# First preparation of a cross-attention and expert kernel written as its own program: new order of stages, weights in halves, output weight in quarters

## The chip, the cores and the metric

The kernel runs on one NeuronCore of a Trainium2 chip. The metric is device time in microseconds (us) of one execution. The kernel before took 869.69 us, the median of three runs (866.67 to 873.19 us).

TensorE (PE) multiplies, VectorE (DVE), ScalarE (ACT) and GpSimd (POOL) do elementwise work, and SyncE (SP) issues most transfers. Each engine works through its own program in order, and the engines meet only in semaphores: an instruction that waits holds up all that stands behind it on its engine.

## The reference, cut to what matters

```python
# B=8 batches, L=112 tokens, D=512, 16 heads of 32; context of 375 rows: 257 image, 118 text
h   = layernorm(x)
q   = rms_norm(h @ q_w.T + q_b) * norm_q_w
k   = rms_norm(ctx_txt @ k_w.T + k_b) * norm_k_w
ki  = rms_norm(ctx_img @ k_img_w.T + k_img_b) * norm_k_img_w
v, vi = ctx_txt @ v_w.T + v_b,  ctx_img @ v_img_w.T + v_img_b
x   = x + (attention(q, k, v) + attention(q, ki, vi)) @ o_w.T + o_b
h   = layernorm(x)                        # then 8 experts, the 2 best of each token:
x   = x + sum_e gate_e * (gelu(gelu(h @ W1_e) @ W2_e) @ W3_e)
```

All is float32 in and out. Products keep float32 accuracy with three matmuls each: every operand is split in a high part, rounded to the type fp32r, and a low part, the rest, and high*high, high*low and low*high are summed.

## The kernel before

**Stages.** `bodies` (L263) runs the body of each engine for b = -1 to 8. In the body of b an engine works on the attention of batch b, on the preparation of batch b + 1 (queries, keys, values), and on the output, gate and routing of batch b - 1. The body of b = -1 holds a preparation alone; that is the first preparation, the one that is changed. After the bodies come the expert blocks, from weights that are loaded as the blocks run. Each body has 16 steps (h = 0 to 15, one per head), and tables say at which step a piece of preparation stands: `FILL` for PE, `EVACUATE_AT` for ACT, `SQUARES_AT` for POOL. The order is written by hand; no scheduler moves anything.

**Names of the preparation.** `xT`: transposes of the normalised x. `qt`, `kt`: the queries (112 tokens) and text keys (118 rows), 12 matmuls of 512 columns each, which ACT copies to `xn` and PE transposes back (`q`, `kx`). `k0` to `k3`: image keys, 12 matmuls of 258 columns each. `v0` to `v2`: values, 12 matmuls of 512 columns each. `ms`: sums over squares for the RMS norm; POOL then raises them to the power -0.5 and `rb` spreads the result. All these tiles of PE go through two PSUM banks in turns (`tile_use`).

**Weights.** Six attention weights of 1 MB arrive as float32 in two buffers (`raw_w`, L167). ACT rounds each to its high part (`split_weights`, L552), DVE subtracts it for the low part (`split_weights`, L734). Their order is image keys, text keys, queries, image values, text values, output (`ORDER`); the first two are split ahead of the body of b = -1, the others in it at steps 2, 7, 11 and 15 (`WEIGHTS_AT`). The context of batch 0 is split by ACT and DVE (L559, L722). On PE the body of b = -1 does k0, k1, kt, kx, xT, qt, k2, q, k3, v0, v1, ms, rb, v2, and last the values of the last image keys (L1238 to L1240), which go to `vlast_d` in memory and come back as one row per batch.

**Other transfers.** SP (from L277) issues weights 1 and 2 with the first context between them, then x of batch 0; each later weight waits until its buffer has been split. Behind these stand x and context of batch 1, then eight stores of zeros (`slots_d`, L313, 528 KB each), and the store of `vlast`. DVE waits for all eight stores at the end of step 0 of batch 0. POOL issues four small loads (`obr`, `wgs`, `bgr`, `b12s`, L399 to L402) at the start.

**The way into batch 0.** DVE finishes the queries and the first chunk of keys (`normalise_queries`, `normalise_keys`, then the low parts into `kq`, L805 and L801), PE makes the first scores (L1140), and DVE takes their maxima (L811), behind which the exponentials of ACT stand.

## Time and profile before

| | |
|---|---|
| median of three runs | 869.69 us (866.67 to 873.19) |
| the profiled execution, its own time | 870.31 us |
| its span in the trace | 868.5 us |
| busy: PE, weight loads of PE, DVE, ACT, POOL | 88%, 77%, 70%, 57%, 27% |
| chain that ended last: PE, DVE, ACT, issue, DMA | 72%, 11%, 7%, 5%, 1% |
| TensorE clock granted, mean | 0.942 of full |

Of each row of the profile the time is the start from the span's begin; "busy" counts instructions, not how full the engine is. The chain of waits is followed back from the last instruction: at each step to what released it. Matmuls are shown with modelled ends, so the distance from one start to the next says more than one's own duration.

### The profile page before, as it was taken

The page shows a single profiled execution, that of the slowest core. Times are in us where ns is not written, and L with a number is a line of the kernel's source. Part 1 is how long each engine was busy: PE and PEld are TensorE (multiplying, and loading weights), DVE is VectorE, ACT ScalarE, POOL GpSimd, SP SyncE. Part 2 cuts the span into 40 slices and gives each one's busy share as a digit, 9 for nine tenths or more (in the row PEclk, how much of TensorE's full clock was granted, in tenths as well). Part 3 has the DMA queues.
Part 4 walks back from the last instruction along what each step waited for, and adds up shares of the span by engine and source line. Part 5 has one row for each costly group of instructions (what it writes and reads, how often), then busy time and mean ns, then how long its engine had stood idle before and what let it go on. Part 6 is the DMA issues. An engine that isn't in the chain of part 4 may idle for free.

```text
span 868.5 us, 17362 instructions
## 1 busy us (share of the span) xinstructions
PE 767.1 (88%) x5934; PEld 668.7 (77%) x5934; DVE 603.7 (70%) x1276; ACT 495.2 (57%) x1131; POOL 231.2 (27%) x286
## 2 busy tenths in 40 slices
PE   3879898999999999764299999999999999999991
PEld 2657676767776767543299999999999999999991
DVE  5476878787878787657166768676767767676853
ACT  4366777777777777682044645554555455454640
POOL 3232334343433333104710303021111112030301
PEclk9999999999999999665599999999999999999996
DMA  6631001020202010405845565656665657565663
GB/s 217 251 135 55 22 38 53 39 65 27 66 26 72 20 43 3 180 21 220 300 157 194 212 216 194 255 174 251 212 247 175 250 198 259 179 246 187 222 213 125
DMA packets 28929, 130.68 MB, mean 150 GB/s; under 512 B 4316, under 2 KB 4332, under 8 KB 17872
## 3 DMA queue, kind: packets, MB, share of 16 engines
q1 hardware_dynamic: 23264, 114.26, 37.3%
q0 software_dynamic: 5616, 15.81, 5.1%
q8 instruction: 26, 0.43, 0.2%
q14 instruction: 23, 0.19, 0.1%
HBM read 113.14 MB, written 19.01 MB: 152 GB/s over the span
## 4 chain that ended last, share of the span: by engine, by line
PE 72%; DVE 11%; ACT 7%; issue 5%; DMA 1%; POOL 1%; SPq 0%; ACTq 0%; DVEq 0%; POOLq 0%
PE tiles L1040 7%; PE tiles L1042 7%; PE tiles L1041 7%; PE scores L1304 4%; PE scores L1302 4%; PE scores L1303 4%; PE ptb L1150 4%; PE ptb L1040 3%; PE ptb L1041 3%; PE ptb L1042 3%; PE pvb L1042 3%; PE pvb L1040 3%; PE pvb L1041 3%; PE pvb L1173 2%; PE scores L1140 2%
## 5 line engine op out<-in xcount | busy, mean ns | idle before, releaser
L834 DVE TENSOR_TENSOR w<-scr,w 128x2048 fp32r<-128x2048 f32 x76 | 174.1, 2291 | 69.9 <-ACT w L624 69.9
L624 ACT ACTIVATE w<-scr 128x2048 fp32r<-128x2048 f32 x76 | 144.8, 1907 | 60.7 <-PE scores L1304 59.3
L470 POOL DMA_INDIRECT out_dram<-scr,tok x18 | 36.5, 2030 | 301.1 <-DVE scr L1030 298.4
L606 ACT ACTIVATE scr<-scr,rsum 112x257 f32<-112x257 f32 x128 | 66.4, 519 | 62.8 <-DVE rsum L818 62.7
L1040 PE MATMUL tiles<-c,w 128*128 128x256 f32 (+1 forms) x272 | 81.3, 299 | 18.1 <-DVE c L722 15.5
L1042 PE MATMUL tiles<-w 128*128 128x256 f32 x288 | 81.5, 283 | 0.0
L1041 PE MATMUL tiles<-w 128*128 128x256 f32 x288 | 81.5, 283 | 0.0
L1040 PE MATMUL tiles<-w 128*128 128x256 f32 x288 | 81.5, 283 | 0.0
L1150 PE MATMUL ptb<-ident,scr 112*128 112x112 f32 x384 | 65.2, 282 | 18.3 <-ACT scr L614 16.6
L1042 PE MATMUL tiles<-c,w 128*128 128x256 f32 (+1 forms) x272 | 78.7, 289 | 0.0
L1041 PE MATMUL tiles<-c,w 128*128 128x256 f32 (+1 forms) x272 | 78.7, 289 | 0.0
L1150 PEld LDWEIGHTS ptb<-ident,scr 112*128 112x128 f32 x384 | 44.5, 149 | 42.5 <-ACT scr L606 26.7
L1018 DVE CAST w<-scr 128x256 fp32r<-128x256 f32 x144 | 44.0, 306 | 43.1 <-ACT scr L690 43.1
L614 ACT ACTIVATE scr<-ptb 128x336 f32<-128x336 f32 x128 | 57.4, 449 | 24.4 <-PE ptb L1150 24.3
L1040 PEld LDWEIGHTS tiles<-c,w 128*128 128x128 f32 x272 | 53.7, 197 | 20.1 <-issue 19.7
L690 ACT ACTIVATE scr<-tiles,b12s 128x256 f32<-128x256 f32 x72 | 33.2, 472 | 57.3 <-PE tiles L1042 57.2
L1020 DVE TENSOR_TENSOR w<-scr,w 128x256 fp32r<-128x256 f32 x144 | 61.3, 426 | 4.9
L598 ACT ACTIVATE scr<-scores,nmax 112x257 f32<-112x257 f32 x128 | 62.3, 486 | 2.5 <-DVE nmax L812 2.5
L1302 PE MATMUL scores<-w 128*128 128x512 f32 x144 | 56.9, 395 | 0.0
L811 DVE TENSOR_REDUCE nmax<-scores 112x2 f32<-112x514 f32 x64 | 44.0, 687 | 18.0 <-PE scores L1140 18.0
L1304 PE MATMUL scores<-w 128*128 128x512 f32 x144 | 56.2, 390 | 0.0
L1303 PE MATMUL scores<-w 128*128 128x512 f32 x144 | 56.1, 390 | 0.0
(214 smaller groups left out, 2291.4 us busy)
## 6 DMA issues: line engine op xcount, KB each, us to landing
scr<-in_dram SPq DMA_DIRECT2D x86, 1024.0 KB, 4.8
scr<-in_dram SPq DMA_DIRECT2D x8, 750.0 KB, 4.6
scr<-slots_d SPq DMA_DIRECT2D x10, 528.0 KB, 3.7
slots_d<-rows SPq DMA_DIRECT2D x8, 528.0 KB, 11.6
xn<-in_dram SPq DMA_DIRECT2D x10, 256.0 KB, 3.1
xb<-in_dram SPq DMA_DIRECT2D x8, 224.0 KB, 2.9
xr<-in_dram SPq DMA_DIRECT2D x8, 224.0 KB, 2.5
out_dram<-x SPq DMA_DIRECT2D x8, 224.0 KB, 2.8
```

Source lines behind the costliest of these rows:

```text
L598: act.activation(probs[0:L, s, 0:IMG], scores[0:L, s, 0:IMG], ACT.Exp, bias=nmax[0:L, g, s, 0:1], accum_out=sums[0:L, g, s, 0:1])
L606: act.activation(probs[0:L, s, 0:IMG], probs[0:L, s, 0:IMG], ACT.Copy, scale=rsum[0:L, g, s, 0:1]).then_inc(S["normal_img"], 1)
L624: act.activation(EH[slot], raw[slot], ACT.Copy).then_inc(S["eh_done"], 1)
L834: dve.tensor_tensor(EL[slot], raw[slot], EH[slot].bitcast(F32), ALU.subtract).then_inc(S["el_done"], 1)
L1020: dve.tensor_tensor(hL[lay][:, c, :], gel[:, m % 4, :], hH[lay][:, c, :].bitcast(F32), ALU.subtract).then_inc(S["hl_done"], 1)
L1040: pe.matmul(out, wh, xh, start=start, stop=False)
L1041: pe.matmul(out, wh, xl, start=False, stop=False)
L1042: return pe.matmul(out, wl, xh, start=False, stop=stop)
L1150: mm = pe.transpose(ptb[:, t * L:(t + 1) * L], probs[0:L, h % 4, t * P:(t + 1) * P], ident[0:L, 0:L])
L1302: pe.matmul(yb[:, t, :], h_hi, wh[:, i, :], start=(f == 0), stop=False)
L1303: pe.matmul(yb[:, t, :], h_hi, wl[:, i, :], start=False, stop=False)
L1304: mm = pe.matmul(yb[:, t, :], h_lo, wh[:, i, :], start=False, stop=(f == 7))
```

## The change

The first preparation is taken out of `bodies` and written as a function `first` for POOL, ACT, DVE and PE, and as straight code for SP; the body of b = -1 is gone.

- Order on PE: xT, qt, kt (half), q, kt, k0, kx, k1, k2, k3, v0, v1 (half), ms, v1, rb, v2.
- Order of the weights: queries, text keys, image keys, image values, text values. They arrive and are split in halves of 512 KB, in three buffers; the third is the start of `scr`, the keys and values of the odd batches.
- SP issues x of batch 0 first, then the query weight, the context, and the rest.
- POOL, not ACT, makes the high part of the first context. Its four small loads stand behind that.
- The output weight is loaded in quarters of 256 KB into `x1` and `rows`, and is split in batch 0: ACT at steps 1, 2, 8 and 9, DVE at steps 2, 3, 9 and 10. Two quarters are issued ahead of the eight stores of zeros, two in batch 0 behind the context of batch 2.
- The values of the last image keys are made in batch 0, step 0, behind the first scores; their store stands there too.
- All squares, adds and norms keep their engines.

The diff, without unchanged lines that say nothing and with the indentation cut by eight; of removed blocks the first two lines stand:

```diff
-ORDER = (WKI, WK, WQ, WVI, WV, WO)
-WEIGHTS_AT = {2: 2, 7: 3, 11: 4, 15: 5}
+ORDER = (WQ, WK, WKI, WVI, WV)
+BIG_FIRST = ("qt", "kt", "k0", "k1", "k2", "k3", "v0", "v1", "v2")
+OUT_HIGH_AT = {1: 0, 2: 1, 8: 2, 9: 3}
+OUT_LOW_AT = {2: 0, 3: 1, 9: 2, 10: 3}
...
-    if b <= FIRST:
+    if b < FIRST:
+        g = BIG_FIRST.index(name)
+    elif b == FIRST:
         g = (each - 1) * (b - FIRST + 1) + i - (i > o)
...
-vlast = rows[0:B, 0, 0:D]
+vlast = xr[0:B, :]
...
-raw_w = [scr[:, probs_at + i * PIECE:probs_at + (i + 1) * PIECE] for i in range(2)]
+raw_w = [scr[:, i:i + PIECE] for i in (probs_at, probs_at + PIECE, 0)]
+raw_o = [x1[:, :], rows[:, 0, 0:D]]
+side = lambda ap, k: ap[:, k * PIECE // 2:(k + 1) * PIECE // 2]
+quarter = lambda ap, c: ap[:, c * D:(c + 1) * D]
...
-    for b in range(-1, DONE + 1):
+    for b in range(FIRST, DONE + 1):
         body(b, b % 2)
...
-has_heads = lambda b: not (fixed(b, -1) or fixed(b, DONE))
+has_heads = lambda b: FIRST <= b <= LAST
...
+    def next_x(b):
+        sp.wait_ge(S["xh_done"], b + 2)
+        sp.dma_start(xb[0:L, :], x[b + 2]).then_inc(S["x_in"], 16)
+    def load_weights(i):
+        for k in range(2):
+            if i >= 3:
+                sp.wait_ge(S["wh_done"], 2 * (i - 3) + k + 1)
+                sp.wait_ge(S["wl_done"], 2 * (i - 3) + k + 1)
+            sp.dma_start(side(raw_w[i % 3], k), side(wT[ORDER[i]], k)).then_inc(wraw_in[i % 3][k], 16)
+    def load_out_weight(c):
+        if c > 1:
+            sp.wait_ge(S["oh_done"], c - 1)
+            sp.wait_ge(S["ol_done"], c - 1)
+        sp.dma_start(raw_o[c % 2], quarter(wT[WO], c)).then_inc(out_in[c % 2], 16)
+    sp.dma_start(xb[0:L, :], x[0]).then_inc(S["x_in"], 16)
+    load_weights(0)
+    sp.dma_start(cr, ctxT[0]).then_inc(S["c_in"], 16)
+    for i in range(1, 5):
+        load_weights(i)
+        if i == 2:
+            sp.dma_start(xlT[:, :, :], ctx_last).then_inc(S["xl_in"], 16)
+    next_x(-1)
+    next_context(-1)
+    sp.wait_ge(S["zeroed"], 1)
+    load_out_weight(0)
+    load_out_weight(1)
+    for e in range(E):
+        sp.dma_start(slots_d[e * REGION:e * REGION + BLOCK, :].rearrange("(p r) d -> p r d", p=P),
+                     rows[:, 1, :].unsqueeze(1).to_broadcast([P, FILLS, ROW])).then_inc(S["zero_stored"], 16)
...
         if has_heads(b):
+            if fixed(b, FIRST):
+                sp.wait_ge(S["vlast_sb"], 1)
+                sp.dma_start(vlast_d, vlast).then_inc(S["vlast_out"], 16)
+                sp.wait_ge(S["vlast_out"], 16)
...
             if b < LAST - 1:
-                sp.wait_ge(S["xh_done"], b + 2)
-                sp.dma_start(xb[0:L, :], x[b + 2]).then_inc(S["x_in"], 16)
+                next_x(b)
                 next_context(b)
+            if fixed(b, FIRST):
+                load_out_weight(2)
+                load_out_weight(3)
...
-    pool.dma_start(obr[:, :], o_b.rearrange("(a d) -> a d", a=1).partition_broadcast(P)).then_inc(S["small_in"], 16)
-    pool.dma_start(wgs[:, :, :], wg).then_inc(S["small_in"], 16)
...
+    def rms_power(b):
+        pool.wait_ge(S["ms_read"], b + 2)
+        pool.tensor_tensor(rr[:, :], msb[:, :], mhalf[:, :], ALU.pow).then_inc(S["r_done"], 1)
+    def first():
+        rstd(1, mv1, ve1, rs1, "ln1")
+        pool.wait_ge(S["c_in"], 16)
+        for i in range(2):
+            pool.tensor_copy(c_part(cH)[i], cr[:, :, PARTS[i]]).then_inc(S[("ch0_done", "ch1_done")[i]], 1)
+        pool.dma_start(obr[:, :], o_b.rearrange("(a d) -> a d", a=1).partition_broadcast(P)).then_inc(S["small_in"], 16)
+        pool.dma_start(wgs[:, :, :], wg).then_inc(S["small_in"], 16)
+        pool.dma_start(bgr[:, :], bg.rearrange("(a d) -> a d", a=1).partition_broadcast(P)).then_inc(S["small_in"], 16)
+        pool.dma_start(b12s[:, :, :], b12).then_inc(S["small_in"], 16)
+        for name in ("q", "k0", "kx", "k1", "k2", "k3"):
+            square(name, -1, 1)
+        rms_power(-1)
+        rstd(2, mv1, ve1, rs1, "ln1")
+        split_queries(0, 0)
+        split_keys(0, 0, 0)
+        split_ctx_high(1, 0)
...
-        if fixed(b, -1):
-            rstd(1, mv1, ve1, rs1, "ln1")
...
-            if h == 0 and has_prep(b) and not fixed(b, -1):
+            if h == 0 and has_prep(b):
                 split_ctx_high(b + 1, 1)
...
-            if h == 1 and has_prep(b) and not fixed(b, -1):
+            if h == 1 and has_prep(b):
                 pool.wait_ge(S["ms_read"], b + 1)
...
-                pool.wait_ge(S["ms_read"], b + 2)
-                pool.tensor_tensor(rr[:, :], msb[:, :], mhalf[:, :], ALU.pow).then_inc(S["r_done"], 1)
+                rms_power(b)
...
+    first()
...
-    def split_weights(i):
-        act.wait_ge(wraw_in[i % 2], 16 * (i // 2 + 1))
...
+    def split_weights(i, k):
+        act.wait_ge(wraw_in[i % 3][k], 16 * (i // 3 + 1))
+        act.activation(side(wH(ORDER[i]), k), side(raw_w[i % 3], k), ACT.Copy).then_inc(S["wh_done"], 1)
+    def split_out_weight(c):
+        act.wait_ge(out_in[c % 2], 16 * (c // 2 + 1))
+        act.activation(quarter(wH(WO), c), raw_o[c % 2], ACT.Copy).then_inc(S["oh_done"], 1)
...
+    def first():
+        for k in range(2):
+            split_weights(0, k)
+        evacuate("xT", -1, 1)
+        for k in range(2):
+            split_weights(1, k)
+        evacuate("qt", -1, 1)
+        for k in range(2):
+            split_weights(2, k)
+        evacuate("kt", -1, 1)
+        split_weights(3, 0)
+        evacuate("k0", -1, 1)
+        split_weights(3, 1)
+        evacuate("k1", -1, 1)
+        act.wait_ge(S["xl_in"], 16)
+        act.activation(xl2[:, 0, :, :], xlT[:, :, :], ACT.Copy).then_inc(S["xlh"], 1)
+        evacuate("k2", -1, 1)
+        split_weights(4, 0)
+        evacuate("k3", -1, 1)
+        split_weights(4, 1)
+        evacuate("v0", -1, 1)
+        evacuate("rb", -1, 1)
+        evacuate("v1", -1, 1)
...
-            if fixed(b, -1) and h in WEIGHTS_AT:
-                split_weights(WEIGHTS_AT[h])
+            if fixed(b, FIRST) and h in OUT_HIGH_AT:
+                split_out_weight(OUT_HIGH_AT[h])
...
-            if fixed(b, -1) and h == 15:
+            if fixed(b, FIRST) and h == 1:
                 act.wait_ge(S["vlast_mm"], 1)
...
                 act.wait_ge(S["vbias_done"], 1)
+    first()
...
-    for i in range(2):
-        dve.memset(kn[i][:, :, KEYS:KP], 0.0)
+    dve.memset(kn[0][:, :, KEYS:KP], 0.0)
     dve.tensor_scalar(ident[:, :], iota[:, :], pidx[:, 0:1], None, ALU.is_equal).then_inc(S["nq_done"], 1)
...
-    def split_weights(i):
-        dve.wait_ge(S["wh_done"], i + 1)
...
+    def split_weights(i, k):
+        dve.wait_ge(S["wh_done"], 2 * i + k + 1)
+        dve.tensor_tensor(side(wL(ORDER[i]), k), side(raw_w[i % 3], k), side(wH(ORDER[i]), k).bitcast(F32),
+                          ALU.subtract).then_inc(S["wl_done"], 1)
+    def split_out_weight(c):
+        dve.wait_ge(S["oh_done"], c + 1)
+        dve.tensor_tensor(quarter(wL(WO), c), raw_o[c % 2], quarter(wH(WO), c).bitcast(F32), ALU.subtract).then_inc(S["ol_done"], 1)
...
+    def first():
+        dve.wait_ge(S["x_in"], 16)
+        ln_stats(1, xb, st1, mv1, "ln1")
+        split_weights(0, 0)
+        ln_apply(1, xb[0:L, :], xb, mv1, rs1, "ln1", "xn_done")
+        split_weights(0, 1)
+        take_x(-1)
+        for i in range(2):
+            split_ctx_low(1, i)
+        for i in range(1, 3):
+            for k in range(2):
+                split_weights(i, k)
+        take_q(-1, 1)
+        split_weights(3, 0)
+        take_kx(-1, 1)
+        split_weights(3, 1)
+        dve.wait_ge(S["xlh"], 1)
+        dve.tensor_tensor(xl2[:, 1, :, :], xlT[:, :, :], xl2[:, 0, :, :].bitcast(F32), ALU.subtract).then_inc(S["xll"], 1)
+        for k in range(2):
+            split_weights(4, k)
+        for i in range(2):
+            add_squares(-1, i)
+        add_sums(-1)
+        take_ms(-1)
+        dve.wait_ge(S["wl_done"], 10)
+        dve.memset(kn[1][:, :, KEYS:KP], 0.0)
+        dve.memset(probs[:, :, KEYS:KT * P], 0.0)
+        dve.wait_ge(S["x_in"], 32)
+        ln_stats(2, xb, st1, mv1, "ln1")
+        normalise_queries(-1, 1)
+        normalise_keys(0, 0)
+        split_queries_low(0, 0)
+        split_keys_low(0, 0, 0)
+        normalise_keys(0, 1)
+        ln_apply(2, xb[0:L, :], xb, mv1, rs1, "ln1", "xn_done")
+        split_ctx_low(2, 0)
...
-            if fixed(b, -1) and h in WEIGHTS_AT:
-                split_weights(WEIGHTS_AT[h])
...
+            if fixed(b, FIRST) and h in OUT_LOW_AT:
+                split_out_weight(OUT_LOW_AT[h])
...
-            if h == 1 and has_prep(b) and not fixed(b, -1):
+            if h == 1 and has_prep(b):
                 split_ctx_low(b + 2, 1)
...
+    first()
...
                 pe.wait_ge(S["xn_done"], n + 1)
-                pe.wait_ge(S["kx_read"], b + 2)
+                if not fixed(b, -1):
+                    pe.wait_ge(S["kx_read"], b + 2)
             else:
+                if name == "kx" and fixed(b, -1):
+                    pe.wait_ge(S["q_read"], 1)
+                if name == "kx" and fixed(b, FIRST):
+                    pe.wait_ge(S["vlast_sb"], 1)
...
-        if fixed(b, -1):
-            pe.wait_ge(S["nq_done"], 3)
...
+            if h == 0 and fixed(b, FIRST):
+                values_of_last_image_keys()
             for name, lo, hi in FILL[h]:
                 if has(name, b):
-                    if fixed(b, -1) and lo == 0 and name in ("kt", "qt", "v0", "v2"):
-                        pe.wait_ge(S["wl_done"], 2 + ("kt", "qt", "v0", "v2").index(name))
                     stage(name, lo, hi, b, p)
...
-            if h == 5 and fixed(b, FIRST):
-                pe.wait_ge(S["wl_done"], 6)
...
+            if h == 15 and fixed(b, FIRST):
+                pe.wait_ge(S["ol_done"], NC)
+    def values_of_last_image_keys():
+        pe.wait_ge(S["xll"], 1)
+        pe.wait_ge(S["rb_read"], 1)
+        wh, wl = wv(WVI)
+        for c in range(NC):
+            pe.matmul(pvb[0:B, :], xl2[:, 0, c, :], wh[:, c, :], start=(c == 0), stop=False)
+            pe.matmul(pvb[0:B, :], xl2[:, 0, c, :], wl[:, c, :], start=False, stop=False)
+            mm = pe.matmul(pvb[0:B, :], xl2[:, 1, c, :], wh[:, c, :], start=False, stop=(c == NC - 1))
+        mm.then_inc(S["vlast_mm"], 1)
+    def first():
+        pe.wait_ge(S["nq_done"], 3)
+        stage("xT", 0, 1, -1, 1)
+        pe.wait_ge(S["wl_done"], 2)
+        stage("qt", 0, NC, -1, 1)
+        pe.wait_ge(S["wl_done"], 4)
+        stage("kt", 0, 2, -1, 1)
+        stage("q", 0, 1, -1, 1)
+        stage("kt", 2, NC, -1, 1)
+        pe.wait_ge(S["wl_done"], 6)
+        stage("k0", 0, NC, -1, 1)
+        stage("kx", 0, 1, -1, 1)
+        for name in ("k1", "k2", "k3"):
+            stage(name, 0, NC, -1, 1)
+        pe.wait_ge(S["wl_done"], 8)
+        stage("v0", 0, NC, -1, 1)
+        stage("v1", 0, 2, -1, 1)
+        stage("ms", 0, 1, -1, 1)
+        stage("v1", 2, NC, -1, 1)
+        stage("rb", 0, 1, -1, 1)
+        pe.wait_ge(S["wl_done"], 10)
+        stage("v2", 0, NC, -1, 1)
+    first()
...
```

## Rows read from the trace of the kernel before

**Rows 1.** Chain of waits, 0 to 52 us: start, us, engine, what is written, line.
```profile
2.58 11.91 DMA xb<-in_dram
...
22.73 0.43 PE tiles L1101
...
27.53 0.64 DVE xs L765
...
29.22 0.23 PE tiles L1100
...
31.54 0.12 PE tiles L1042
...
34.61 0.48 ACT scr L590
...
37.41 2.20 DVE w L736
...
39.77 1.03 POOL rr L516
...
45.10 1.37 DVE kq L801
46.46 0.40 DVE scr L750
...
47.11 2.21 DVE w L736
...
49.48 0.42 DVE xb L732
49.90 1.14 DVE c L722
51.04 0.60 DVE nmax L811
```
**Rows 2.** Timeline of PE: start, us, line, operation, tile, count, idle before and releaser.
```profile
19.59 0.57 PE L1100 MATMUL tiles<-w,c 128*118 128x512 f32 x1 [2.11 <-DVE w L736]
...
49.10 0.79 PE L1140 MATMUL scores<-kq 32*112 32x376 f32 x12 [0.68 <-ACT rows L661]
...
58.50 0.78 PE L1140 MATMUL scores<-kq 32*112 32x376 f32 x12
```
**Rows 3.** Timeline of ACT, the same columns.
```profile
6.47 1.91 ACT L554 ACTIVATE w<-scr 128x2048 fp32r<-128x2048 f32 x1 [4.46 <-DMA scr<-in_dram]
...
71.21 0.45 ACT L614 ACTIVATE scr<-ptb 128x336 f32<-128x336 f32 x1 [1.68 <-PE ptb L1150]
```
**Rows 4.** Timeline of POOL, the same columns.
```profile
16.45 0.61 POOL L428 TENSOR_TENSOR scr<-scr 128x257 f32<-128x257 f32 x1
19.17 3.14 POOL L428 TENSOR_TENSOR scr<-scr 128x257 f32<-128x257 f32 x1 [2.12 <-ACT scr L590]
...
45.01 1.04 POOL L452 CAST c<-scr 128x1032 fp32r<-128x1032 f32 x1
```
**Rows 5.** Stretches: length, busy PE, PEld, DVE, ACT, POOL, granted clock, DMA share, GB/s.
```profile
6.50:10.00 3.50, 0.00 (x0) 0.00 (x0) 1.59 (x1) 1.88 (x1) 0.00 (x0) 1.00 1.03 246
...
18.00:22.00 4.00, 2.41 (x6) 1.88 (x7) 3.85 (x3) 1.10 (x2) 2.83 (x1) 0.73 0.30 82
...
42.00:46.00 4.00, 4.00 (x19) 2.84 (x18) 3.46 (x8) 2.51 (x3) 2.52 (x3) 1.00 1.06 391
```
**Rows 6.** Stretches of batches 0 and 1, the same columns.
```profile
49.00:90.00 41.00, 35.29 (x298) 27.26 (x298) 28.84 (x80) 28.97 (x103) 13.04 (x19) 0.96 0.14 48
90.00:131.00 41.00, 37.59 (x342) 29.33 (x341) 32.29 (x89) 31.16 (x108) 14.76 (x24) 1.00 0.09 32
```
**Rows 7.** Issues by line and tile, with the time from issue to landing.
```profile
L313 SPq DMA_DIRECT2D slots_d<-rows x8: 630/922/2400, 33.0 to 40.6; - x8
...
DMA to landing us min/median/max: 9.2/11.6/12.3
```
**Rows 8.** Issues of the whole run: size of one, median us from issue to landing.
```profile
xb<-in_dram SPq DMA_DIRECT2D x8, 224.0 KB, 2.9
```

More of the change, by code:

```diff
@@ L234, in cross_attention_moe @@
         S = {n: sem(n) for n in (
[L235 removed]
+            "vec_in", "oh_done", "ol_done", "small_in", "aggr", "held", "wh_done", "wl_done", "xl_in", "xlh", "xll", "consts", "zeroed", "zero_stored",
             "vbias_done", "nq_done", "vlast_mm", "vlast_sb", "vlast_out",
@@ L248, in cross_attention_moe @@
         tile_free = [sem(f"tile_free{i}") for i in range(2)]
-        wraw_in = [sem(f"wraw_in{i}") for i in range(2)]
+        wraw_in = [[sem(f"wraw_in{i}{k}") for k in range(2)] for i in range(3)]
+        out_in = [sem(f"out_in{i}") for i in range(2)]
         raw_in = [sem(f"raw_in{i}") for i in range(4)]
@@ L305, in body @@
                     if b < LAST - 1:
-                        sp.wait_ge(S["xh_done"], b + 2)
-                        sp.dma_start(xb[0:L, :], x[b + 2]).then_inc(S["x_in"], 16)
+                        next_x(b)
                         next_context(b)
-                if fixed(b, -1):
-                    sp.wait_ge(S["zeroed"], 1)
-                    for e in range(E):
-                        sp.dma_start(slots_d[e * REGION:e * REGION + BLOCK, :].rearrange("(p r) d -> p r d", p=P),
-                                     rows[:, 1, :].unsqueeze(1).to_broadcast([P, FILLS, ROW])).then_inc(S["zero_stored"], 16)
-                    sp.wait_ge(S["vlast_sb"], 1)
-                    sp.dma_start(vlast_d, vlast).then_inc(S["vlast_out"], 16)
-                    sp.wait_ge(S["vlast_out"], 16)
+                    if fixed(b, FIRST):
+                        load_out_weight(2)
+                        load_out_weight(3)
                 if fixed(b, LAST):
@@ L706, in _ @@
                 dve.memset(half[1][:, :, 0:1].bitcast(F32), 0.0)
-            for i in range(2):
-                dve.memset(kn[i][:, :, KEYS:KP], 0.0)
+            dve.memset(kn[0][:, :, KEYS:KP], 0.0)
             dve.tensor_scalar(ident[:, :], iota[:, :], pidx[:, 0:1], None, ALU.is_equal).then_inc(S["nq_done"], 1)
@@ L1229, in body @@
                         pe.wait_ge(S["small_in"], 64)
-                    if h == 5 and fixed(b, FIRST):
-                        pe.wait_ge(S["wl_done"], 6)
-                if fixed(b, -1):
-                    pe.wait_ge(S["xll"], 1)
-                    pe.wait_ge(S["rb_read"], 1)
-                    wh, wl = wv(WVI)
-                    for c in range(NC):
-                        pe.matmul(pvb[0:B, :], xl2[:, 0, c, :], wh[:, c, :], start=(c == 0), stop=False)
-                        pe.matmul(pvb[0:B, :], xl2[:, 0, c, :], wl[:, c, :], start=False, stop=False)
-                        mm = pe.matmul(pvb[0:B, :], xl2[:, 1, c, :], wh[:, c, :], start=False, stop=(c == NC - 1))
-                    mm.then_inc(S["vlast_mm"], 1)
-                    pe.wait_ge(S["vlast_sb"], 1)
+                    if h == 15 and fixed(b, FIRST):
+                        pe.wait_ge(S["ol_done"], NC)
```

35 lines of the change are left out of this document (removed).

## The prediction

> **What bounds the kernel now.** I read the profile in this order: the page's busy shares, the chain of waits up to 52 us, the timelines of PE, ACT and POOL, the stretches, the DMA issues. The change touches only what lies ahead of batch 0 and batch 0 itself, so the question is when batch 0 can start and how long it takes.
>
> The chain [rows 1] first goes through a transfer: x of batch 0 lands at 14.5 us, because it stands behind two weights and a context on the queue. Then come the text keys, which wait for their low weights on DVE and run from 19.6 us [rows 1, 2]; the queries only after them; and the last image keys, whose copy on ACT is at 34.6 us. From there a serial tail leads to the scores: square, adds, sums, power, spread, normalising, split; the last low part of the keys ends at 46.5 us. PE then still does the values of the last image keys, and makes the first scores at 49.1 us [rows 2]. DVE does not read them at once: a whole weight (2.21 us), the norm and a context split stand ahead, and the maxima start at 51.04 us [rows 1]. Batch 0 then takes 40.9 us and batch 1 41.0, with PE busy for 35.3 and 37.6 us [rows 6]: batch 0 has some room, as it has no output projection.
>
> **The path of the changed kernel, step by step.** Half a weight costs ACT 1.91 / 2 = 0.95 us [rows 3] and DVE 2.21 / 2 = 1.1 to 1.2 us [rows 1].
>
> *Start.* x is the second issue, at about 1.2 us, and lands some 2.9 us later [rows 8]: 4.1 us. A full weight landed at 6.4 us [rows 3]; the first half, behind x, at about 5.6. ACT 6.6, DVE 7.8, the normalised x at 8.6, four transposes, copy and low part (0.64 us, [rows 1]) until about 10.5. The queries start at 10.6 us.
>
> *Queries and text keys.* The matmuls before 23 us come every 0.43 us, those at 29 us every 0.23 us [rows 1]: 1.2 and 2.4 GHz, and the stretch from 18 to 22 us shows a granted clock of 0.73 after an idle time of 2.1 us [rows 2, 5]. So I cost the 12 matmuls of the queries at 4.5 us, to 15.1. The context lands at 9 to 10 us. POOL casts it in 1.04 us and about 0.6 [rows 4], in place of 1.56 us on ACT, DVE takes 1.8 us for the low parts to 13.1, and both halves of the text weight until 15.4 us. Text keys 15.5 to 18.9, with the query transposes inside.
>
> *Image keys.* ACT copies the queries at 15.1 to 15.7 and only then rounds image halves: 16.7, 17.7; DVE 19.1. k0 starts at 19.2; four tiles of 12 matmuls at 0.12 us [rows 1] and the transposes kx end at 25.6 us. The image weight itself is there by 15 us: 4.15 MB at about 0.38 MB per us from 3 us on, the rate of [rows 5] at 42 us (391 GB/s), so no transfer holds this.
>
> *Tail.* ACT copies k3 at 25.7 (34.6 before). With DVE busy on the last weight, the square ends at 27.5 and the adds start after that weight, at 28.7; from the start of the copy to the end of the sums it took 2.8 us (34.61 to 37.41, [rows 1]) and takes 4.9 now. But the 2.20 us of weight between the sums and the power (at 37.41, [rows 1]) is gone. Sums 30.6, power (1.03 us, [rows 1]) 32.9, spread 33.6, ACT 34.2, low keys at 38.5 with the same collision with the context cast as before (1.37 us, [rows 1]). v0, v1 and v2 fill PE meanwhile, to 36.4. **First scores at 38.7 us**, not 49.1.
>
> *Maxima.* Ahead of them now stand keys 1 (0.40 and 0.25), the norm (0.42) and the context split (1.14, [rows 1]): **41.1 us, not 51.04: 9.9 us earlier**. The last weight's 2.21 us on DVE has left this place.
>
> *Batch 0 gives back.* PE does 12 matmuls of 0.23 us, 2.8 us, behind the first scores. Before, PE waited there 1.3 us for DVE, and the next wait, for the context split about 4 us behind the maxima, hides the rest: k1 ends at 45.1 where the split ends at 45.4. ACT gets the copy of these values (0.45) and two quarters (0.95 in all) in front of the fourth exponential: 1.4 us, of which PE's own queue to the second scores (58.5 us, [rows 2]) hides about 1. Loss 0.4. At step 8 ACT waits for the third quarter, which lies behind x and the context of batch 2: landing near 70.5 in old time, where ACT waited for PE until 71.21 anyway, idle for 1.68 us [rows 3]; with the quarter and the held normalising I take 0.7. Quarters at step 9 on ACT and at 9 and 10 on DVE: 0.3. Sum 1.4 us. With cover gone these are worth at most 2.8 on PE and 1.9 + 0.45 on ACT; below, 0.
>
> *Edits at nothing.* POOL's four small issues, moved behind the context cast, end near 15 us; POOL next has the squares of the queries at 19.7, and their data is wanted after 42 us. The zero stores: now issued from about 17 us. All bytes to their end are 12.4 MB (two x 0.46, five weights 5.25, two contexts 1.54, small 0.35, two quarters 0.52, stores 4.3), at 0.38 MB per us until 36 to 38 us; DVE asks at about 43. They took 11.6 us each from issue to landing [rows 7]. SP's `vlast` store and row load (a few us) end by 47 us; the first product with values comes at about 54. The third buffer lets two weights wait in store; the order of tiles is already in the path above.
>
> *Unknown costs.* No row shows a 512 KB load in two halves. Bounds: nothing (the eight 528 KB stores run at 391 GB/s, [rows 5]), and the slowest loaded stretch, 246 GB/s while the small loads ran [rows 5], which would bring the image weight at 20 us instead of 15, 3 us late for ACT. I take nothing, as the stores are nearest in size. The Trainium skill (DMA: Bandwidth & Descriptors, Bandwidth) asks for transfers of 1 MiB and more for 75% of peak, and so speaks against the halves; by its fit of 64 KB and 1 MB the ten halves would cost about 3 us of stream, of which the path would feel 1. The stores of half that size in [rows 5] do not bear it out.
>
> **Sum.** 9.9 - 1.4 = 8.5 us. The profiled execution took 870.31 us, 0.6 above the median of 869.69, so 861.2 to 861.8: **861.5 us**.
>
> **The rivals.**
> (a) *Batch 0 gives back more*: ACT and PE are in turns on the chain there, and every added instruction counts: 2.8 + 0.45 + 1.9 = 5.2, gain 4.7, 865.5 us. For: ACT and DVE are each busy 29 of 41 us and meet PE at each group of heads. Against: PE is busy only 35.3 [rows 6]. 0.15.
> (b) *POOL is held by DVE*: a square of 0.61 us took 3.14 us when it ran beside DVE's weight split [rows 4]. In the new order the context cast and five squares stand beside such splits. If the cast and the squares of k2 and k3 each lose 2 us, the first scores come 2 to 4 us later: gain 4.5 to 6.5, 864.5. The Trainium skill (SBUF, shared port pair) says that a DVE instruction with two SBUF inputs locks POOL's reads out for its length; by that rule this case is the likely one, and the trace agrees with the mechanism. Halves shorten each lock to 1.15 us, which is why I put most of it inside the sum. 0.13.
> (c) *The path is shorter than mine* by 2 to 3 us (context at 9 us, batch 0 giving nothing back): 858. 0.12.
> (d) *The stores of zeros or a weight come late*: if they land as late as before, about 51 us, DVE is held at the end of step 0 until then, 8 us: 868 us. 0.05.
> (e) *Slower: the clock stays low.* Place: PE's first preparation. If waits of about 2 us keep coming, as the one ahead of 19.59 us [rows 2], all its matmuls up to k3 run at 1.2 GHz: text keys 2.8 and image keys 5.7 us more, and the values ahead of the sums 4.2, together 12.7: 4 us slower, 874. It decides from 8.5 us of lost pace on. Against: behind the wait for DVE at 27.5 us the matmuls at 29.2 us came every 0.23 us [rows 1]. 0.05.
>
> **How the numbers follow.** Forecast 0.50, within 858.5 to 864.5. About 1% (8.7 us, so 861.0) is what this kernel's measurement can tell from no change. The forecast lies just on the near side of that line: a little under half of it, (c) and hardly any other count as faster, 0.23 + 0.12 + 0.03 of runs' scatter = 0.40; slower (e) and a part of what I haven't seen, 0.05; within 1%, 0.55. The range, 856 to 867.5, leaves out (d), (e) and the ends of the others, about 2 in 10.
>
> **What would show it.** Queries start near 10.6 us; k0 at 19; ACT's copy of k3 at 25.7; first scores at 38.7, maxima at 41.1; second scores 9.5 us earlier than 58.5; batch 1 begins 8.5 us earlier; from there on the same lengths. Wrong it would be if k0 starts after 22 us (transfers, clock or POOL, to be read from the releaser), if DVE stands still at the end of step 0 for the stores, or if batch 0 takes over 43.5 us.

## The result, and the profile after

The changed kernel takes 863.89 us (median of 8 runs, 862.01 to 864.45), the kernel before, measured in the same rounds, 870.22 us (866.67 to 874.62). The ratio is 0.9917 with a 95% interval of 0.9893 to 0.9942: 0.8% faster, 6.3 us between the medians, 7.2 us between the means. The forecast was 861.5 us, range 856 to 867.5, and 8.5 us of gain. The profiled execution took 863.47 us, with a span of 861.6 us (868.5 before).

The chain of waits of the changed kernel, 0 to 52 us (start, us, engine, what is written, line):

```profile
1.64 4.41 DMA scr<-in_dram
6.08 1.06 ACT w L598
7.16 1.23 DVE w L800
8.39 0.47 DVE xb L796
...
8.99 0.99 PE pvb L1160 x4
...
10.58 0.64 DVE xs L824
...
11.36 0.74 PE tiles L1198
...
16.65 0.96 ACT w L598
17.63 2.38 DVE w L800 x2
20.05 0.39 PE tiles L1133
...
26.53 0.48 ACT scr L630
27.01 0.95 ACT w L598
27.98 1.34 DVE w L800
...
37.92 1.36 DVE kq L860
...
40.71 1.14 DVE c L786
41.85 0.60 DVE nmax L870
```

Read it against [rows 1]. The 11.91 us of transfer for x are gone: the chain starts with half a query weight, which ACT has from 6.08 us. Queries start at 11.36 us, image keys at 20.05, the copy of k3 is at 26.53 where it was at 34.61, and the maxima are at 41.85 where they were at 51.04. The whole weight on DVE that stood ahead of them (47.11) is no longer there.

The first and second scores on PE answer to [rows 2]:

```profile
39.43 0.77 PE L1238 MATMUL scores<-kq 32*112 32x376 f32 x12 [2.33 <-DVE kq L860]
...
50.21 0.77 PE L1238 MATMUL scores<-kq 32*112 32x376 f32 x12
```

Batch 0 and batch 1 of the changed kernel, from first scores to first scores (length, busy PE, PEld, DVE, ACT, POOL, granted clock, DMA share, GB/s), answer to [rows 6]:

```profile
39.00:83.00 44.00, 38.11 (x310) 28.28 (x310) 32.18 (x85) 30.82 (x106) 13.55 (x19) 0.96 0.13 41
83.00:124.00 41.00, 37.57 (x342) 29.34 (x341) 32.43 (x89) 31.22 (x108) 14.29 (x24) 1.00 0.09 32
```

Batch 0 grew from 40.9 to 43.5 us (39.43 to 82.95) as PE, DVE and ACT took over work, so a part of the lead is given back there. That is just the length that the prediction named as a sign of being wrong (over 43.5 us); in a second trace of the same kernel it was 45.1 us (39.94 to 85.06).

**How the lead is followed from here on.** For every group of four heads I take the start of DVE's first maxima in both traces and subtract. For the changed kernel the lead is 9.2, 8.3, 8.3 and 7.0 us in the four groups of batch 0, and 7.0 in all of batch 1. The first maxima repeat to about 0.5 us between two traces of this kernel (41.78 and 42.29); the leads behind them differ by 1.3 to 2.8 us in batch 0, by the clock (experiment 1). Whole runs of one kernel scatter by 2 to 8 us.

### The profile page after: what moved, and what is told of

Its sections match the earlier page's. It is cut to its first block, busy times and chain, and to the rows that moved or that the text cites. A ratio compares the mean times of both kernels' runs of the same rounds, so it can differ in the third digit from the quotient of the medians.

```text
span 861.6 us, 17388 instructions
## 1 busy us (share of the span) xinstructions
PE 766.7 (89%) x5934; PEld 667.6 (77%) x5934; DVE 606.8 (70%) x1284; ACT 494.9 (57%) x1137; POOL 232.2 (27%) x288
## 4 chain that ended last, share of the span: by engine, by line
PE 73%; DVE 10%; ACT 9%; issue 5%; DMA 1%; POOL 1%; SPq 0%; ACTq 0%; DVEq 0%; POOLq 0%
PE tiles L1133 7%; PE tiles L1135 7%; PE tiles L1134 7%; PE scores L1422 4%; PE scores L1420 4%; PE scores L1421 4%; PE ptb L1248 4%; PE pvb L1134 3%; PE pvb L1133 3%; PE ptb L1134 3%; PE ptb L1133 3%; PE ptb L1135 3%; PE pvb L1135 3%; PE scores L1238 2%; PE pvb L1271 2%
## 5 line engine op out<-in xcount | busy, mean ns | idle before, releaser
L1133 PE MATMUL tiles<-c,w 128*128 128x256 f32 (+1 forms) x272 | 79.9, 294 | 4.6 <-DVE c L1097 2.6
L1135 PE MATMUL tiles<-c,w 128*128 128x256 f32 (+1 forms) x272 | 77.5, 285 | 0.0
L1134 PE MATMUL tiles<-c,w 128*128 128x256 f32 (+1 forms) x272 | 77.4, 284 | 0.0
```

The source lines that it names most:

```text
L1133: pe.matmul(out, wh, xh, start=start, stop=False)
L1134: pe.matmul(out, wh, xl, start=False, stop=False)
L1135: return pe.matmul(out, wl, xh, start=False, stop=stop)
```

## The experiments

Each ratio is to the kernel before in the same rounds. Its median was 869.57 us for experiments 2 to 4, 872.17 us for 5 and 7 to 9, and 870.31 us for 6 and 10 to 12, so ratios can be compared between experiments, and times only within one of these groups. What is read from a trace rests on one trace of each kernel, two of the changed one.

**1. A second trace of the changed kernel.** No edit.

> The changed kernel once more, unchanged, for a second trace. If the 2 us that were lost between batches 1 and 3 in the first trace (granted clock 0.83 at 120 to 130 us and 0.9 at 160 to 180 us, where the kernel before shows 1.00) belong to the change, they are there again at the same places; if they are chance, they lie elsewhere or are missing, and the span moves by 1 to 2 us.

Measured: 863.26 us, span 861.4. Maxima at 42.29. Lead 8.7, 7.0, 5.5, 4.9 in batch 0, then 4.9 to 5.0 until batch 3, where the next 1 us goes. The first trace lost 1 us at the start of batch 2 (7.0 to 6.0) and 1 us at the start of batch 3 (6.0 to 5.0). The first of these is missing here, so it is chance. The second is there again at the same place, with 0.83 granted from 165 to 175 us in both traces, so this run doesn't show it to be chance; experiments 2 to 7, 11 and 12 have no fall of the clock there. What differs between the two traces is the clock. Stretches of this trace:

```profile
40.00:45.00 5.00, 5.00 (x25) 2.16 (x26) 4.96 (x12) 1.69 (x7) 2.13 (x2) 0.67 0.00 0
55.00:60.00 5.00, 3.29 (x34) 2.50 (x35) 2.89 (x9) 4.46 (x16) 1.51 (x3) 0.70 0.35 83
60.00:65.00 5.00, 5.00 (x26) 3.45 (x24) 0.66 (x3) 1.50 (x4) 0.18 (x1) 0.62 0.74 271
120.00:130.00 10.00, 8.75 (x77) 6.10 (x76) 8.46 (x25) 5.99 (x21) 3.25 (x5) 1.00 0.08 23
```

and of the first trace of the same kernel:

```profile
55.00:60.00 5.00, 3.98 (x35) 2.91 (x35) 3.01 (x10) 3.46 (x12) 1.05 (x3) 0.66 0.69 229
120.00:130.00 10.00, 9.02 (x70) 6.68 (x59) 9.17 (x25) 5.10 (x17) 3.15 (x5) 0.83 0.08 23
```

The granted clock fell at 40 us in one and stayed full in the other, fell at 60 us again in the one, and at 120 us in the other. Such a fall costs 0.8 us of lead at 40 us (1.65 lost up to the second group, 0.89 without it), 1.5 at 60 us and 1.0 at 120 us. PE waited alike ahead of the first: 2.33 us before the scores at 39.43 in the first trace, 2.31 us before those at 39.94 in the second. So the same wait can be followed by a fall or not, in two executions of the same program.

**2. The quarters issued early.**

```diff
+                    if fixed(b, FIRST):
+                        load_out_weight(2)
+                        load_out_weight(3)
                     if b < LAST - 1:
                         next_x(b)
                         next_context(b)
-                    if fixed(b, FIRST):
-                        load_out_weight(2)
-                        load_out_weight(3)
```

> The changed kernel with the third and fourth quarter of the output weight issued at the head of batch 0, before x and the context of batch 2 (nothing else moved). Theory (the wait at step 8 is on the path): ACT's wait for the third quarter, 1.93 us of idle time ending at 62.7 us, is gone, and batch 1 starts about 1.3 us earlier against the first maxima than in the changed kernel: the lead over the kernel before stays at 8.3 us at the fourth scores in place of 7.0, and the time is 1 to 1.5 us under the changed kernel's 863.9. Rival (the added splits themselves cost, not the transfer): the lead still falls from 8.3 to about 7.2 between the third and fourth scores.

Measured: 862.73 us, ratio to before 0.9903 (0.9866 to 0.9941). ACT's wait is gone, as the timelines of ACT show, the changed kernel first:

```profile
62.74 0.63 ACT L602 ACTIVATE w<-x 128x512 fp32r<-128x512 f32 x1 [1.93 <-DMA x<-in_dram]
```

```profile
61.46 0.62 ACT L602 ACTIVATE w<-x 128x512 fp32r<-128x512 f32 x1
```

Between the third and fourth group the lead fell by 0.6 us instead of 1.3: the transfer was worth about half of the loss, the added splits the other. At the end of batch 0 the lead is still 7.0: it fell by 1.65 us over the first group, where 0.89 is lost without a fall of the clock, and this trace has 0.70 granted from 40 to 45 us. The time did not move by more than the scatter.

**3. The last values back in the first preparation.** PE's `values_of_last_image_keys()` behind v2 in `first`, ACT's copy behind that of v1, and both gone from batch 0.

> The changed kernel with the values of the last image keys at the end of the first preparation on PE (behind v2) and their copy there on ACT, as before the change. Theory: PE waits 2.33 us ahead of the first scores in the changed kernel, so the 12 matmuls (2.8 us) push the scores by at most 0.6 us and the maxima, which DVE's own work holds at 41.8, by nothing; batch 0 gets rid of 0.45 us on ACT and 2.8 on PE, and the lead at the second scores is 8.7 to 9.2 in place of 8.3. Rival: the place makes no difference at all because ACT's two quarters set the second scores: lead 8.3 to 8.5.

Measured: 863.58 us, ratio 0.9911 (0.9874 to 0.9949). Scores 40.24, 0.8 us later where 0.6 at most was foreseen, and maxima 41.91: as foreseen, they cost DVE's path next to nothing in either place. Lead 9.1, 8.6, 7.6, 6.9: 0.5 us is lost to the second scores in place of 0.9, which lies between theory (8.7 to 9.2) and rival (8.3 to 8.5). The clock was at half from 55 to 60 us (0.50 granted, 0.66 in the changed kernel), to which I put the rest. As a whole their place makes no difference that can be measured.

**4. The output weight in the gaps of the first preparation.**

```diff
-ORDER = (WQ, WK, WKI, WVI, WV)
+ORDER = (WQ, WK, WKI, WVI, WV, WO)
...
+                for k in range(2):            # ACT, behind v0
+                    split_weights(5, k)
...
                 add_sums(-1)
+                split_weights(5, 0)           # DVE
                 take_ms(-1)
...
                 ln_stats(2, xb, st1, mv1, "ln1")
+                split_weights(5, 1)           # DVE
                 normalise_queries(-1, 1)
```

> The changed kernel with the output weight as a sixth weight of the first preparation, in halves through the third buffer: ACT rounds them behind v0, where it idles for 4.5 us, DVE takes one half between the sums and the mean square (idle 1.15 us) and one between the statistics of batch 1 and the norm of the queries (idle 1.5 us). No quarters in batch 0. Theory: the first maxima stay at 41.8 to 42.2, batch 0 gives back only what the last values cost, lead at the fourth scores 8.5 to 9, time about 862. Rival (DVE is full after all, or the weight lands late behind the stores): the maxima move to 43 to 44 and nothing is won, about 864.

Measured: **860.65 us**, ratio 0.9871 (0.9832 to 0.9910), the lowest ratio of all, though its interval overlaps that of the changed kernel and those of experiments 11 and 12. Maxima 41.65; lead 9.3, 9.3, 9.1, 9.1 in batch 0, then 9.1 to 9.2 up to batch 3. This trace has the same clock in batch 0 as the first of the changed kernel (one fall, 0.66 from 55 to 60 us), so the two can be set side by side: 2.2 us given back against 0.2. By this pair the quarters in batch 0 cost 2 us, and the same work costs nothing where ACT and DVE idle for the RMS norm. Experiments 11 and 12 have no quarters in batch 0 either, and their traces still give back 2.4 and 2.7 us there, with the clock down at 40 us (0.66) and from 55 to 60 us (0.50): one trace alone would not tell the quarters from the clock.

**5. Whole weights.** One load, one ACT and one DVE instruction for each weight, all else as in the changed kernel.

```diff
-                dve.wait_ge(S["wh_done"], 2 * i + k + 1)
-                dve.tensor_tensor(side(wL(ORDER[i]), k), side(raw_w[i % 3], k), side(wH(ORDER[i]), k).bitcast(F32),
-                                  ALU.subtract).then_inc(S["wl_done"], 1)
+                if k == 0:
+                    dve.wait_ge(S["wh_done"], i + 1)
+                    dve.tensor_tensor(wL(ORDER[i]), raw_w[i % 3], wH(ORDER[i]).bitcast(F32),
+                                      ALU.subtract).then_inc(S["wl_done"], 1)
```

> The changed kernel with whole weights of 1 MB in place of halves: one load, one ACT and one DVE instruction for each, in the order and the three buffers of the changed kernel. Theory (halves only shorten the latency from landing to the low part): the query weight lands near 7 us, is low at 11.3, the queries start at 11.5 to 12.5 us and not 11.36; ACT's first copy of x is not held; k0 waits 1.91 + 2.28 us behind the copy of the queries and starts about 1 to 1.5 us later than 20.05; first maxima 43.5 to 44.5 in place of 41.8. Rival (fixed cost of small transfers, by which whole loads arrive earlier): image values and values arrive earlier and the maxima are at 41 to 42.

Measured: 869.88 us, ratio 0.9963 (0.9924 to 1.0002): about half of the gain is gone by the ratio, and what is left is no longer clear of the scatter. Maxima at 48.47, 6.7 us later, where 2 to 3 were foreseen. Its chain of waits:

```profile
1.64 5.92 DMA scr<-in_dram
7.58 1.92 ACT w L598
9.53 3.14 DVE w L801
12.67 0.73 DVE xb L796
13.54 1.00 PE pvb L1161 x4
```

The normalised x stands behind the low part on DVE. In halves it slips in at 8.4 us; whole, it waits until 12.7. The expectation had overlooked that x itself is ready at 6 us and held only by its place in DVE's program. The 3.14 us are those of a 2.29 us instruction that met POOL's cast of the context, which is two instructions:

```profile
9.48 1.04 POOL L517 CAST c<-scr 128x1032 fp32r<-128x1032 f32 x1 [3.61 <-DMA scr<-in_dram]
...
10.47 2.64 POOL L517 CAST c<-scr 128x472 fp32r<-128x472 f32 x1
```

DVE started at 9.53, just behind the first cast, and took 0.85 us more than alone; the second cast, 0.58 us in the changed kernel, took 2.64. In experiment 6 DVE started at 10.05, when the first cast (9.18, 1.04 us) was nearly done, and took 2.32. The Trainium skill (SBUF — State Buffer, SBUF: two separate sides) says that of a DVE instruction with two inputs in SBUF and a POOL instruction that reads SBUF, the one that starts first holds the shared ports for its whole length and the other waits; the traces agree, in both directions.

**6. Whole weights, norm first.**

```diff
-                split_weights(0, 0)
                 ln_apply(1, xb[0:L, :], xb, mv1, rs1, "ln1", "xn_done")
-                split_weights(0, 1)
+                split_weights(0, 0)
                 take_x(-1)
```

and on ACT the copy of the transposes ahead of the query weight.

> The kernel with whole weights (e3) with the norm and the transposes of x taken out from behind the query weight: DVE applies the norm ahead of the low part of the query weight, ACT copies the transposes ahead of rounding it. Theory (halves win mostly because the norm slips in between two halves; whole, it stood behind 3.14 us of low part until 12.59): x is normalised near 6.1 us, but ACT's copy now delays its rounding little, the query weight is low at about 11.8, queries start at 12 in place of 15.9, and the first maxima come at 44.5 to 45.5 in place of 48.47; the rest to 41.8 is the latency of whole image weights. Rival (the size of a load is what costs): queries start at 14 or later, maxima at 47 or more.

Measured: 865.21 us, ratio 0.9946 (0.9929 to 0.9964). x normalised at 5.97, queries 13.05, k0 23.04, maxima 45.56 us. So of the 6.7 us that halves are worth at the maxima, 2.9 are the place of the norm, and 3.8 the latency of whole weights. The queries start 1.7 us later than at 11.36. From there to k0 it takes 1.3 us more: 0.5 in the queries themselves, more of which run at half pace, and 0.8 from their copy to k0, where a whole image weight costs 1.90 + 2.29 us in a row and two halves 0.96 + 2.38. From k0 to the copy of k3 it takes another 0.7, since that copy stands behind 1.91 us of rounding the last weight (28.46) on ACT. In time, halves are worth less than in the maxima: by the ratios 0.3% against whole weights with the norm first and 0.5% with the norm behind; both intervals touch the changed kernel's.

**7. The context back on ACT.** ACT makes the high part of context 0 behind the copy of x; POOL's four small loads are then issued at 6.0 us and not at 11.4.

> The changed kernel with the high part of the first context back on ACT (behind the copy of x, ahead of the text weight), POOL's four small issues then at about 6 us. Theory (the context is no longer on the path, the query matmuls cover it): k0 starts within 0.5 us of 20.05, maxima within 0.7 us of 41.8. Rival (DVE held POOL's cast and it mattered): the cast of 2.19 us becomes 1.56 on ACT and text keys and maxima come 0.5 to 1 us earlier; the other way, the small packets of the small loads slow the weights and everything comes 1 us later.

Measured: 865.59 us, ratio 0.9913 (0.9872 to 0.9953), which does not differ from the changed kernel's 0.9917. Maxima 42.65, 0.9 us later; text keys 17.62 in place of 15.86, k0 20.89. It was the second thing in the rival, not POOL's speed. Timeline of ACT, this kernel and then the changed one, at the second half of the text weight:

```profile
15.25 1.06 ACT L595 ACTIVATE w<-scr 128x1024 fp32r<-128x1024 f32 x1 [1.85 <-DMA scr<-in_dram]
```

```profile
12.01 1.06 ACT L598 ACTIVATE w<-scr 128x1024 fp32r<-128x1024 f32 x1 [0.22 <-DMA scr<-in_dram]
```

With the small loads ahead, that half arrives 3.2 us later than in the first trace of the changed kernel, and 2.5 us later than in the second (12.79). Two things were changed here at once; the wait named is the transfer's.

**8. The kernel before with x first.** x is issued ahead of the first weight, nothing else.

> The kernel before with one thing changed: x of batch 0 is issued first, ahead of the weights. Theory (the late x held DVE only, and only for 1.4 us, before the text weight): text keys start 1.5 to 2 us before 19.59, the first maxima 1 to 2 us before 50.96, time 1 to 1.5 us less. Rival (the chain's 11.9 us of transfer is a cause by itself, and its removal gives most of what the change gives): maxima 5 us or more earlier.

Measured: 872.53 us, ratio 0.9986 (0.9946 to 1.0027); text keys 19.55, maxima 50.91. Nothing, where 1 to 2 us were foreseen: the first weight now lands at 8.91 us in place of 6.47, DVE has its low part at 13.1 and comes to the statistics of x at 14.77, as late as ever (14.52). So the 11.9 us of transfer at the head of the chain in [rows 1] were the last of several waits to end, and not 11.9 us of cause.

That it is exactly nothing is in part the clock of this trace. PE waited only 0.69 us ahead of the text keys, not 2.11 [rows 2], did them at full pace, and began the queries at 26.68 us, 1.6 earlier than 28.30. Within them the clock fell to half (0.76 granted from 25 to 30 us), and the 1.6 us were gone by the first image keys behind them (31.08, 31.14 before):

```profile
26.68 0.45 PE L1100 MATMUL tiles<-w,xs 128*112 128x512 f32 x1 [1.39 <-DVE xs L765]
...
27.69 0.63 PE L1101 MATMUL tiles<-w,xs 128*112 128x512 f32 x1
28.11 0.63 PE L1102 MATMUL tiles<-w,xs 128*112 128x512 f32 x1
```

Whether x first is worth up to 1.6 us where the clock stays full is open; the four runs show no gain in time.

**9. The kernel before with the output weight later.** The quarters of the changed kernel in batch 0, no sixth weight in the first preparation.

> The kernel before with one thing changed: the output weight in quarters in batch 0, as in the changed kernel, and no sixth weight in the first preparation. Theory: DVE loses 2.2 us ahead of the maxima but the scores stay at 49.1 behind the last values, so the maxima move from 50.96 to about 49.8, gain 1.1; batch 0 gives back about 1.3 for the added splits and the wait for the third quarter; net 0 (870). Rival (the weight on DVE was worth its full 2.2 us and batch 0 hides the quarters): 2 us less, 868.

Measured: 875.11 us, ratio 1.0022 (0.9977 to 1.0066). Scores 49.22, maxima 50.04: 0.9 us earlier (1.1 foreseen). Lead 0.9, 0.4, 0.3, -0.85: batch 0 gives back 1.8 us. Alone, this part loses about 1 us up to batch 1 in this trace; two falls of the clock further on (0.73 at 130, 0.67 at 175 us) make it 2.8. In the time no difference from the kernel before is shown.

**10. Image keys first.** The new form with the old order of stages: weights in the order image keys, text keys, queries; PE does k0, k1, kt, kx, xT, qt, k2, q, k3.

> The changed kernel with the old order of the stages: weights in the order image keys, text keys, queries, image values, text values; PE does k0, k1, kt, kx, xT, qt, k2, q, k3; halves, three buffers, the late small loads, the context on POOL and the work moved to batch 0 stay. Theory: k0 starts near 13 us at half clock, but the queries wait for the third weight and for kx to be read, start at 23 to 24 us, and the last image keys are copied 3 us later than in the changed kernel: maxima 44 to 46 in place of 41.8. Rival (the order is worth nothing, since PE has the same work and halves feed it): maxima at 41 to 43.

Measured: 869.87 us, ratio 0.9991 (0.9971 to 1.0012). Maxima 48.69, lead in batch 0 2.3, 1.4, 1.4, 0.5. In this one schedule of the old order, written by hand, all the rest of the change is worth 2.3 us at the maxima and nothing in the time. PE stands idle around the transposes as before (24.88, 26.34 and 28.30 us there); only the 2.11 us ahead of the text keys are gone:

```profile
13.41 0.55 PE L1132 MATMUL tiles<-c,w 128*128 128x258 f32 x1 [13.41 <-DVE c L785]
22.24 0.62 PE L1156 MATMUL pvb<-ident,xn 118*128 118x118 f32 x4 [0.69 <-ACT xn L625]
23.69 0.57 PE L1156 MATMUL pvb<-ident,xb 112*128 112x112 f32 x4 [0.83 <-DVE scr L833]
25.65 0.74 PE L1194 MATMUL tiles<-w,xs 128*112 128x512 f32 x1 [1.38 <-DVE xs L823]
```

x goes through PE only behind the text keys, the queries start at 25.65 us and at half clock, and k2 and k3 stand behind them: the copy of k3 is at 33.38. The foreseen 3 us were 6.9. Some 2.3 of them are pace: k0 and k1, now the first matmuls, come every 0.215 us (24 from 13.41 to 18.6 us) and not every 0.12, and the queries run at half clock in either kernel.

**11. Norm first, image weight ahead (on top of experiment 4).** DVE applies the norm ahead of the first half, ACT copies the transposes between the halves and rounds the image weight ahead of the copy of the queries.

> The version with the output weight in the gaps of the first preparation (e6), and two orders changed: DVE applies the norm of x ahead of the query weight and ACT copies its transposes between the two halves; ACT rounds both halves of the image weight ahead of the copy of the queries (it idles there for 2.98 us). Theory: queries start near 10.2 us in place of 11.4, k0 near 19 in place of 19.9, maxima at 40.3 to 40.9 in place of 41.65, time 1 us under that version. Rival (the image weight hasn't landed, so that ACT holds the copy of the queries behind it): k0 at 20 or later, nothing won or 0.5 us lost.

Measured: 862.72 us, ratio 0.9897 (0.9861 to 0.9932). Queries 11.42, k0 19.92, maxima 41.68: nothing. ACT's copy pushed the second half to 8.60, and its low part met POOL's cast (1.69 us in place of 1.22), so the queries wait for the weight and not for x. The image weight was there in time (13.49 and 14.77), but the copy of the queries came at 16.92 and PE was then the bound. The rival named the wrong cause of the right outcome. Against experiment 4 the time is no better (0.9897 and 0.9871, the intervals overlap).

**12. POOL's context cast earlier (on top of experiment 11).**

```diff
+                split_ctx_high(1, 0)
                 split_queries(0, 0)
                 split_keys(0, 0, 0)
-                split_ctx_high(1, 0)
```

> The version before this one (e10) with POOL's high part of the second context moved ahead of the high parts of queries and keys, and ACT's copy of v1 ahead of that of the RMS factors so that POOL may begin. Theory (the cast of 1.04 us collides with DVE's low part of the keys, 1.36 us instead of 0.54, and with the norm of keys 1): both run at their own pace, and the maxima come 0.7 to 1.2 us earlier than in e10. Rival (DVE and POOL then meet one step earlier, at the norm of the queries, 1.07 us): the queries' norm becomes 1.5 to 2 us and nothing is won.

Measured: 860.32 us, ratio 0.9884 (0.9851 to 0.9917), maxima 41.46. The rival holds. DVE in this kernel, the norm of the queries and the low part of the keys:

```profile
34.40 2.11 DVE L841 SCALAR_TENSOR_TENSOR qn<-qn,nq,rms 128x112 f32<-128x112 f32 x4 [0.29 <-ACT rms L609]
...
38.39 0.89 DVE L855 TENSOR_TENSOR kq<-scr,kq 128x376 fp32r<-128x376 f32 x1 [0.39 <-POOL kq L455]
```

and in the kernel of experiment 11:

```profile
34.87 1.07 DVE L841 SCALAR_TENSOR_TENSOR qn<-qn,nq,rms 128x112 f32<-128x112 f32 x4 [0.29 <-ACT rms L609]
...
37.82 1.36 DVE L855 TENSOR_TENSOR kq<-scr,kq 128x376 fp32r<-128x376 f32 x1 [0.40 <-POOL kq L455]
```

The collision moved from the keys to the queries and costs 1.04 us there, about the 1.05 us of the cast, against 0.47 that it gives back at the low part and 0.33 at the norm of keys 1 behind it: 0.2 us lost. That the maxima are 0.2 us earlier all the same comes from ahead of the edit, where the first half landed at 5.40 and not 5.77, and k0 started 0.5 us earlier (19.45, 19.92).

## Why the prediction was right, point by point

*The path.* The mechanism was the one forecast. Every station came 0.4 to 0.9 us after its forecast and in the order foreseen: queries 11.36 (10.6), text keys 15.86 (15.5), k0 20.05 (19.2), copy of k3 26.53 (25.7), scores 39.43 (38.7), maxima 41.78 in DVE's timeline (41.1). The offset arises ahead of the queries: the first half landed at 6.08 and not 5.6, and the four transposes took 0.98 us, where the same four took 0.59 us at 26.34 us in the kernel before. They ran at half pace, like all matmuls up to 15 us (512 columns every 0.43 us), although the stretches of the profile show 1.00 granted there; for this first part the pace tells the level, 1.2 GHz, and the granted clock does not. Gain at the maxima 9.2 us against 9.9.

*What it is made of* was not told apart in the prediction. Without the order of stages the maxima are at 48.7, without the halves at 48.5, with both at 41.8. They don't add: without the one or the other the lead is only 2.3 and 2.5 us, and not 9.2. The halves are not necessary, though: whole weights with the norm first give 45.6 and a ratio of 0.9946. The clock has no net share in the 9.2: before, the text keys ran mostly at half pace (4.5 us from 19.59) and the queries at full (2.8 us from 28.30), and now it is the queries at half (4.5 us from 11.36) and the text keys at full. x first alone gives nothing, the output weight later alone 0.9 at the maxima and nothing in the time. The third buffer was not tried alone.

*Batch 0 gives back 1.4.* The mis-sized term: it gives back 2.2 (lead 9.2 to 7.0) in the first trace, and 3.7 in the second (8.7 to 4.9), where the clock fell twice more. To the second scores 0.9 and not 0.4, at steps 8 and 9 1.3 and not 1.0. Of the 0.9, 0.5 are left with the last values gone (experiment 3), and nothing with the quarters gone (experiment 4). The room that I read in PE's busy time [rows 6] does not cover work on ACT in front of an exponential. Forecast 8.5 at the end of batch 0, measured 7.0; the wait for the third quarter was in the sum (0.7), and experiment 2 gives about 0.7. The sign of being wrong, a batch 0 over 43.5 us, was barely met in one trace (43.52) and clearly in the other (45.1); it points at this term.

*Edits at nothing.* The zero stores: DVE did not wait for them; the last transfers end by 38 us. The small loads on POOL: more than nothing at the maxima, 0.9 us by experiment 7, but not seen in the time. The 512 KB loads: nothing lost; the stream ran at 379 GB/s from 6.5 to 10 us and at 410 from 10 to 14.

*The rivals.* (a), more given back, is partly true, by 0.8 us in one trace and 2.3 in the other, of the 3.8 it had over the sum. (b), POOL held by DVE, is there in both directions (the last weight's low part 1.34 us, the keys' 1.36): the context cast took 2.19 us, three of the squares 3.19 and the last 1.16, together some 2 us over their pace where nothing meets them (rows of 0.61 and 0.97 us before), and not 6. (c) did not come, the path was 0.7 us longer. (d) and (e) did not come; no idle time of PE ahead of k3 dropped the clock. One sum of the chances is off: 0.23 + 0.12 + 0.03 is 0.38 and not 0.40.

*The end.* Lead 7.0 at batch 1, 5.0 at batch 5, 6.9 at the end. From there on the same lengths, the prediction said; 2 us were lost and 2 us came back, and in the second trace 4.9 at batch 1, 4.1 at batch 6 and 7.1 at the end. That these cancel, so that the end lies 6.9 and 7.1 us ahead, is luck. Behind the bodies the first expert matmul comes 5.1 us earlier (425.10 against 430.20 us), and then the clock rises earlier: 0.70 granted in the first 5 us against 0.50. The kernel before:

```profile
430.00:435.00 5.00, 4.80 (x22) 4.80 (x23) 0.00 (x0) 1.74 (x2) 3.70 (x6) 0.50 0.55 213
```

and the changed kernel:

```profile
425.00:430.00 5.00, 4.90 (x30) 4.90 (x31) 0.05 (x1) 1.84 (x3) 3.82 (x6) 0.70 0.56 215
```

That these gains and losses of 1 to 2 us are chance is shown for the 1 us of batch 2 (experiment 1) and not for that of batch 3, which both traces have; for the expert blocks it is argued from the clock alone.

## What to carry to other kernels

In a first stage that transfers feed, cut what stands ahead of short critical work on an in-order engine: 2.9 of the 6.7 us of the halves came from a short norm that got through between them, which moving the norm gives as well, and the rest from the shorter way from landing to low part. Before moving work out of a busy place, look for the idle spans that the stage has anyway; the output weight cost 2 us in batch 0 and nothing beside the RMS norm, in two traces of like clock. The transfer at the head of a chain of waits can be only the last of several waits that end together: issue it first, alone, and see, and look at the clock of the trace before the result is believed.

## What the runs showed of the hardware that I had not expected

- Two executions of one program grant the clock differently: full at 40 us in one and 0.67 in the other, 0.83 at 120 us in the first and 1.00 in the second. One such fall moved everything behind it by 0.8 to 1.5 us, as much as the edits that were to be told apart.
- Small loads ahead of weights delay them far beyond their bytes: 0.35 MB issued at 6 us in place of 11.4 made half a text weight 2.5 to 3.2 us later. At 390 GB/s, 0.35 MB is 0.9 us.
- DVE and POOL slow each other in both directions, and which one pays hangs on who starts first: a 2.29 us low part took 3.14 when it started 0.05 us behind POOL's cast and 2.32 when it started 0.87 us behind it, a 1.07 us norm took 2.11, and POOL's second cast of 0.58 us took 2.64.
- Up to 15 us the matmuls came at half pace while the profile shows 1.00 granted.
